# Eight products of 128 moving columns in place of two of 512 in a graph kernel's edge stage

## The chip, the cores and the metric

The kernel runs on one core of a Trainium2 chip. The metric is the device time of one execution in microseconds (us). The engines that matter here are TensorE (PE in the profile, its weight loads shown apart as PEld), VectorE (DVE), ScalarE (ACT) and SyncE (SP), which issues the DMAs.

## What is computed

Four graph layers over 512 nodes, each with 512 features. The 8192 edges (`src`, `dst`, sorted by `dst`) are the same in all of them. The part that matters here is what the edges give to each layer: layer 0 is sparse attention with 8 heads and one bias per edge and head, the others add or average neighbours.

```python
x, src, dst, edge_attr_8              # (512,512), (8192,), (8192,), (8192,8)
scores = einsum('ehd,ehd->eh', q[row], k[col]) * scale + bias
m = segment_max(scores, row);  p = exp(scores - m[row])
alpha = p / segment_sum(p, row)[row]
out = segment_sum(alpha[:, :, None] * v[col], row)
...
agg = segment_sum(x[src], dst)        # the later layers: the same edges, unweighted
```

## The kernel before

The kernel turns the edge list into dense 512x512 matrices, one for each of the 8 heads (the sum of exp(bias) over the edges from one node to another) and one with the count of edges. After that everything is dense products. The dense matrices are made in the **edge stage**, and the change is in it.

The edges come in 64 tiles of 128. The destination nodes come in 37 blocks of 14 (`BW`). A **slot** is one tile of edges meeting one block; there are 100 slots, in 25 groups of 4 (`GROUP`). For a slot the kernel needs, for each of the block's 14 nodes and 9 quantities (8 heads and the count, `KW`), a row over all 512 source nodes: 14 x 9 = 126 rows (`BROWS`). TensorE makes them as a product over the slot's 128 edges. The stationary side (126 columns, loaded as weights) holds each edge's weights in the place of its destination; it exists twice, as a high and a low part for precision (a = 0, 1). The moving side is a one-hot matrix, 128 edges x 512 sources. Both are fp32r. So a slot is two products, of the two stationary sides with the same 512 moving columns, summed in the same PSUM bank. In the profile the moving side is called `wide_rounded` and the stationary side `c_rounded`.

Which PSUM bank a slot adds to depends on its block, known only at run time. TensorE's sequencer reads the block numbers of two groups into registers (`choices`, L1379), waits until the block's bank has been cleared (`evacuated`), and computes the bank's address (an ALU operation and a fused register operation).

VectorE builds the operands: `one_hots` (L792, four per group) and `left_sides` (L798, one per group), in a ring of two groups (`RING`). It may write a ring place once the products that read it are done (`pair_mm`), and TensorE waits for `built` at each group. ScalarE copies each finished block out of PSUM (L483), clears its bank (L488), and SyncE writes the copy to its place by DMA (L287).

TensorE mixes into this stage the query, key and value projections (`qkv_step`, L1373): 48 plain fp32 products of 512 columns, each in the trace as two MATMUL records of two passes. The list `qkv_group` says after which group how many of them come: 7, 4, 3, then 2 after each of 13 groups, then 0, 2, 0, 2, 0, 2, 0, 2. So late in the stage two groups follow one another with no projection between them. The last group runs in a loop (one trip here) that ends with small table products. Behind the stage TensorE computes attention scores (L1447), transposes (L1461) and weighted sums (L1476), and then the rest of the layers.

Ahead of the stage the transposes of z (L1415) are copied out by ScalarE (L459), and the first projection waits for all four copies; the products of group 0 stand in that wait.

Of the kernel before, what the change touches and what calls it, by code (L numbers as in the profile page):

```python
# [24 lines left out]
NT = N // P  # L25
# [39 lines left out]
def gnn_kernel(nc, x, src, dst, bias, eps, cols, rows, wq, wk, wv, wo, w1_0, w2_0,  # L65
               wl_t, wr_t, w1_2, w2_2, w1_3t, w2_3t, out):
    ctx = ExitStack()
    with ctx:
# [76 lines left out]
        for name, words in (("mask", SLOTS * BW), ("bias", HP * P), ("src", P), ("dst", P), ("low", P),  # L145
# [24 lines left out]
        st_ring = c1_r[:, :, :].rearrange("p t n -> p (t n)")[:, 0:RING * GROUP * 2 * BROWS].rearrange(  # L170
            "p (g a w k) -> p g a w k", g=RING, w=BW, k=KW)
        hot_ring = wide_r[:, 0:RING * GROUP, :].rearrange("p (g s) n -> p g s n", g=RING)
# [1016 lines left out]
        def _(pe):  # L1189
            def tile(ap, t):  # L1190
                return ap[:, t * P:(t + 1) * P]
# [106 lines left out]
            def ks(a, n=NT):  # L1298
# [17 lines left out]
                             stop=True).then_inc(S["ends_mm"], 1)  # L1316
# [67 lines left out]
            def pairs(g, u, held):  # L1384

                pe.wait_ge(S["built"], g + 1)
                for k in range(GROUP):
                    pe.wait_ge(S["evacuated"], held[k])
                    to = acc[0:BROWS, bass.ds((held[k] & (ACC - 1)) * N, N)]
                    for a in range(2):  # L1390
                        last = nc.tensor.matmul(to, st_ring[:, u, 2 * k + a, :, :].rearrange("p w k -> p (w k)"),  # L1391
                                                hot_ring[:, u, k, :], start=False, stop=False, skip_group_check=True)
                    last.then_inc(S["pair_mm"], 1)

            def zeros(banks):
# [16 lines left out]
            for i, t in enumerate((0, 2, 1, 3)):  # L1412
                pe.wait_ge(*((S["z_ready"], t + 1) if t < 2 else (S["z_scalar"], t - 1)))
                for c in range(NT):
                    last = nc.tensor.transpose(tile(bank[Z_BANKS[c]], t), tile(z_sb[:, t, :], c), ident[:, :])  # L1415
                    if i == NT - 1:
                        last.then_inc(S["turned"], 1)
            for g in range(NG - 1):
                pairs(g, g % RING, held[GROUP * (g % 2):GROUP * (g % 2 + 1)])
                if g == 0:  # L1420
                    pe.wait_ge(S["t_ready"], NT)
                if g == 1:
                    pe.wait_ge(S["weights_read"], 1)
                for n, after in enumerate(qkv_group):
                    if after == g:
                        qkv_step(n)
                if g % 2 == 1 and g < NG - 2:
                    held = choices((g + 1) * GROUP, 2 * GROUP)
                if g == 2:
                    pe.wait_ge(S["ends_ready"], 1)  # L1430
                    trips = pe.value_load(rounds_i[0:1, 0:1], min_val=1, max_val=MAX_TRIPS)
            with nc.tensor.Fori(0, trips) as j:
                pe.wait_ge(S["rows_ready"], j + 1)
                pe.sem_inc(S["pair_steps"], 1)
                pairs(j + (NG - 1), 0, choices(FIXED))
                pe.wait_ge(S["qkv_ready"], LAST_V[0])
                pair_table(j + 1, slice(FIXED, SLOTS))
# [68 lines left out]
            for t in range(NT):  # L1506
                pe.wait_ge(S["att_ready"], 2 * NT - 1 if t == NT - 1 else 2 * t + 2)
                for c in range(NT):
                    if t == NT - 1 and c == NT // 2:
                        pe.wait_ge(S["att_ready"], 2 * NT)  # L1510
                    last = nc.tensor.transpose(tile(bank[c], t), tile(z_sb[:, t, :], c), ident[:, :])
# [24 lines left out]
            for k in range(NT):  # L1536
                pe.wait_ge(*reads("h1")[k][0])
                for i in range(2):
                    for m in range(NT):
                        nc.tensor.matmul(bank[m][:, :], tile(h1[k][0], m), c1s[k][i], start=(k == 0 and i == 0),  # L1540
                                         stop=False)
            pe.wait_ge(S["h_ready"], 2 * NT)
            turn(h_sb, 4, "turned")
            for k in range(NT):
                pe.wait_ge(*reads("h1")[k][1])
                for m in range(NT):
                    last = nc.tensor.matmul(bank[m][:, :], tile(h1[k][1], m), c1s[k][0], start=False,
                                            stop=(k == NT - 1))
# [102 lines left out]
```

## Time and profile before

| what | value |
|---|---|
| time, median of 2 runs (lowest to highest) | 397.99 us (396.95 to 399.02) |
| span of the profiled execution | 395.7 us |
| PE busy | 371.7 us (94%), 1781 matmuls |
| PEld busy | 282.1 us (71%), 1781 loads |
| DVE busy | 313.2 us (79%) |
| ACT busy | 171.5 us (43%) |
| L1391, the products of the slots | 200 matmuls, 58.2 us busy |
| L1373, the projections | 96 matmul records, 44.5 us busy |
| mean granted TensorE clock | 0.992 |

The span is that of one profiled execution, from its first to its last instruction; the runs' median is 2.3 us above it. A matmul's recorded duration is its latency, and consecutive matmuls overlap in the records. What one costs in a dense row is therefore the distance from one start to the next and not the mean duration.

### The profile page before, as it was taken

To read this page: it belongs to the slowest core of one execution; us is meant where nothing else is said; L and a number is where in the kernel's file an instruction comes from. 1 tells how busy PE (TensorE), PEld (TensorE's weight loads), DVE (VectorE), ACT (ScalarE), POOL (GpSimd) and SP (SyncE) were. 2 spreads that over 40 slices of the span, in tenths; PEclk is the share of its full clock that TensorE was granted. 3 is DMA by queue.
4 is the path that set the end of the run, shared out by engine and by line. 5 is a ranking of instruction groups with operands and counts; after the bars stand their busy time and mean duration, and the time that the engine had idled before them with its cause. 6 is when DMAs were issued, how large, how long until landed. Compare 5 with 4: busy or idle time off the path is not lost.

```text
span 395.7 us, 5097 instructions
## 1 busy us (share of the span) xinstructions
PE 371.7 (94%) x1781; PEld 282.1 (71%) x1781; DVE 313.2 (79%) x660; ACT 171.5 (43%) x287; POOL 4.2 (1%) x19
## 2 busy tenths in 40 slices
PE   2889999999988999999989999999799999999994
PEld 1555666666757888887768788887578878787873
DVE  5889999999947779997886978499875778488346
ACT  5664666444136224343467723361363531135320
POOL 4000000000000000000000000000000000000000
PEclk9999999999998999999999999999999999999998
DMA  7602444343226000056500230400420032000002
GB/s 240 247 1 69 157 154 135 104 133 110 73 85 208 2 2 1 2 188 243 206 2 1 100 114 14 198 2 0 134 81 0 2 116 96 2 0 0 2 2 104
DMA packets 16360, 32.92 MB, mean 83 GB/s; under 512 B 1360, under 2 KB 1488, under 8 KB 16336
## 3 DMA queue, kind: packets, MB, share of 16 engines
q1 hardware_dynamic: 15744, 32.25, 23.6%
q10 hardware_dynamic: 592, 0.36, 0.3%
q8 instruction: 15, 0.25, 0.3%
q14 instruction: 9, 0.07, 0.1%
HBM read 21.07 MB, written 1.05 MB: 56 GB/s over the span
## 4 chain that ended last, share of the span: by engine, by line
PE 78%; DVE 14%; ACT 4%; issue 3%; DMA 1%; DVEq 0%; ACTq 0%
PE acc L1391 11%; PE bank L1373 10%; PE bank L1476 7%; PE bank L1270 6%; PE bank L1271 6%; PE bank L1251 4%; PE acc L1251 4%; PE acc L1271 4%; PE acc L1270 4%; PE bank L1461 4%; PE acc L1447 3%; DVE big_rounded L652 2%; PE acc L1228 2%; PE bank L1228 2%; PE acc L1540 2%
## 5 line engine op out<-in xcount | busy, mean ns | idle before, releaser
L1391 PE MATMUL acc<-wide_rounded,c_rounded 128*126 128x512 f32 x200 | 58.2, 435 | 0.7 <-ACT acc L464 0.7
L1391 PEld LDWEIGHTS acc<-wide_rounded,c_rounded 128*126 128x126 f32 x200 | 37.2, 187 | 17.8 <-issue 10.7
L792 DVE TENSOR_SCALAR wide_rounded<-iota_f,picked 128x512 fp32r<-128x512 f32 x100 | 42.6, 482 | 2.1 <-issue 1.1
L483 ACT COPY z_sb<-acc 126x512 f32<-126x512 f32 x37 | 21.6, 585 | 44.9 <-PE acc L1391 36.2
L507 ACT ACTIVATE wide<-wide,low_col 128x512 f32<-128x512 f32 x32 | 21.3, 715 | 32.8 <-DVE low_col L905 32.8
L1476 PEld LDWEIGHTS bank<-v_sb,big 128*128 128x128 f32 x256 | 29.7, 192 | 4.7 <-issue 4.3
L625 DVE TENSOR_TENSOR wslot_rounded<-wslot,wide_rounded 128x512 fp32r<-128x512 f32 x24 | 16.2, 688 | 21.3 <-ACT wslot L377 21.3
L1476 PE MATMUL bank<-v_sb,big 128*128 128x65 f32 x256 | 31.6, 277 | 0.0
L798 DVE TENSOR_TENSOR c_rounded<-row_bc,wslot_rounded 128x1008 fp32r<-128x1008 bf16 x25 | 30.0, 1201 | 0.0
L1373 PE MATMUL bank<-t_sb,wslot 128*128 128x512 f32 x64 | 29.5, 594 | 0.5 <-ACT t_sb L459 0.5
L652 DVE TENSOR_TENSOR big_rounded<-big,big_rounded 128x1024 fp32r<-128x1024 f32 x24 | 29.1, 1222 | 0.4
L369 ACT ACTIVATE std<-mv,eps_c 128x1 f32<-128x1 f32 x20 | 5.8, 290 | 39.4 <-DVE mv L657 25.9
L905 DVE CUSTOM_DVE_ANT_0 wide<-acc,t_sb 128x512 f32<-128x512 f32 x32 | 20.7, 684 | 1.7 <-PE acc L1447 1.6
L917 DVE TENSOR_TENSOR big<-bank,big 128x512 f32<-128x512 f32 x32 | 20.6, 684 | 1.4 <-PE bank L1461 1.4
L1461 PE MATMUL bank<-ident,wide 128*128 128x128 f32 x128 | 18.3, 285 | 2.7 <-ACT wide L507 2.7
L1373 PEld LDWEIGHTS bank<-t_sb,wslot 128*128 128x128 f32 x64 | 12.0, 189 | 11.5 <-issue 9.6
L488 ACT COPY acc<-zero_c 126x512 f32<-126x512 f32 x33 | 19.4, 588 | 1.0
L1271 PE MATMUL acc<-big_rounded,wslot_rounded 128*128 128x512 f32 x48 | 18.7, 389 | 0.0
L1270 PE MATMUL acc<-big_rounded,wide_rounded 128*128 128x512 f32 x48 | 18.7, 389 | 0.0
L1461 PEld LDWEIGHTS bank<-ident,wide 128*128 128x128 f32 x128 | 15.0, 151 | 4.2 <-ACT wide L507 3.6
L374 ACT ACTIVATE wide_rounded<-bank,col 128x512 fp32r<-128x512 f32 x12 | 8.3, 694 | 17.4 <-PE bank L1271 17.4
L1373 PE MATMUL bank<-wslot,t_sb 128*128 128x512 f32 x32 | 15.0, 592 | 0.0
(314 smaller groups left out, 768.8 us busy)
## 6 DMA issues: line engine op xcount, KB each, us to landing
big<-z_sb SPq DMA_DIRECT2D x36, 252.0 KB
big<-in_w SPq DMA_DIRECT2D x4, 2048.0 KB, 7.8
x_sb<-in_x SPq DMA_DIRECT2D x8, 256.0 KB, 4.7
big<-in_w_3t SPq DMA_DIRECT2D x2, 1024.0 KB, 6.8
row_bc<-in_rows SPq DMA_DIRECT2D x7, 256.0 KB, 6.6
wslot<-in_wq SPq DMA_DIRECT2D x1, 1024.0 KB, 8.9
wslot<-in_wk SPq DMA_DIRECT2D x1, 1024.0 KB, 10.8
wslot<-in_wv SPq DMA_DIRECT2D x1, 1024.0 KB, 12.8
```

The costliest lines, as they stand in the source:

```text
L483: nc.scalar.copy(stage[0:BROWS, b % STAGES, :], a).then_inc(S["staged"], 1)
L507: nc.scalar.activation(e, e, ACT.Exp, bias=low_col[:, n // 4, h:h + 1], scale=-1.0).then_inc(S["e_ready"], 1)
L652: nc.vector.tensor_tensor(lo.rounded[:, part, :], lo.full[:, part, :], hi.rounded[:, part, :].bitcast(F32), ALU.subtract).then_inc(S[name ...
L792: nc.vector.tensor_scalar(hot_ring[:, u, k, :], iota_f[:, :], picked[:, 0, s0 + k:s0 + k + 1], None, ALU.is_equal)
L798: nc.vector.tensor_tensor(st_ring[:, u, :, :, :], mask[:, c, :, :].rearrange("p s a w -> p (s a) w").unsqueeze(3).broadcast_to([P, 2 * GRO ...
L1251: nc.tensor.matmul(bank[banks[m]][:, :], tile(a[0], m), r[0], start=(k == 0 and not started), stop=False)
L1270: nc.tensor.matmul(bank[b][:, :], tile(a[0], m), r[1], start=False, stop=False)
L1271: last = nc.tensor.matmul(bank[b][:, :], tile(a[1], m), r[0], start=False, stop=(k == len(terms) - 1))
L1373: ins = nc.tensor.matmul(to[:, :], left, right, start=(k == 0), stop=(k == NT - 1))
L1391: last = nc.tensor.matmul(to, st_ring[:, u, 2 * k + a, :, :].rearrange("p w k -> p (w k)"), hot_ring[:, u, k, :], start=False, stop=False, ...
L1461: last = nc.tensor.transpose(tile(bank[4 + a], t), tile(held_e[:, i % HELD, :], t), ident[:, :])
L1476: last = nc.tensor.matmul(o, by_head[:, t, h, m * P:(m + 1) * P], v_sb[:, t, h, :], start=(t == 0), stop=(t == NT - 1))
```

## The change

The two products of a slot become eight. The 512 source columns are cut into four tiles of 128; for each tile the two stationary sides are multiplied with the tile's 128 moving columns, into the same 128 columns of the same bank. The same sums are made. The order is tile outside, side inside, so the stationary side alternates from product to product. The semaphore update stands on the slot's last product, as before. Nothing else is changed.

```diff
                 for k in range(GROUP):
                     pe.wait_ge(S["evacuated"], held[k])
                     to = acc[0:BROWS, bass.ds((held[k] & (ACC - 1)) * N, N)]
-                    for a in range(2):
-                        last = nc.tensor.matmul(to, st_ring[:, u, 2 * k + a, :, :].rearrange("p w k -> p (w k)"),
-                                                hot_ring[:, u, k, :], start=False, stop=False, skip_group_check=True)
+                    for t in range(NT):
+                        for a in range(2):
+                            last = nc.tensor.matmul(tile(to, t),
+                                                    st_ring[:, u, 2 * k + a, :, :].rearrange("p w k -> p (w k)"),
+                                                    tile(hot_ring[:, u, k, :], t), start=False, stop=False,
+                                                    skip_group_check=True)
                     last.then_inc(S["pair_mm"], 1)
```

On TensorE, at the last slot of group 0 and the projections behind it (L1391 is the slot's product, L1373 a projection; REGISTER_ALU and ISA are the sequencer's register operations that give the bank's address), before:

```order
L1391 REGISTER_ALU
L1391 ISA
L1391 MATMUL acc<-wide_rounded,c_rounded 126x512 x2
L1373 MATMUL bank<-t_sb,wslot 128x512 x7
L1391 REGISTER_ALU
```

and of the change, at the same place:

```order
L1392 REGISTER_ALU
L1392 ISA
L1392 MATMUL acc<-wide_rounded,c_rounded 126x128 x2
L1392 ISA
L1392 MATMUL acc<-wide_rounded,c_rounded 126x128 x2
L1392 ISA
L1392 MATMUL acc<-wide_rounded,c_rounded 126x128 x2
L1392 ISA
L1392 MATMUL acc<-wide_rounded,c_rounded 126x128 x2
L1373 MATMUL bank<-t_sb,wslot 128x512 x7
L1392 REGISTER_ALU
```

Each slot has six more products and three more register operations, since each tile's address is worked out on its own. The projections keep their place. The instructions of the other engines keep their order.

## Rows read from the trace of the kernel before

**Rows 1.** Page, costliest groups: busy us, mean ns of one, idle before it

```profile
L1391 PE MATMUL acc<-wide_rounded,c_rounded 128*126 128x512 f32 x200 | 58.2, 435 | 0.7 <-ACT acc L464 0.7
L1391 PEld LDWEIGHTS acc<-wide_rounded,c_rounded 128*126 128x126 f32 x200 | 37.2, 187 | 17.8 <-issue 10.7
```

**Rows 2.** Chain that ended last, in order of time: start us, us, what

```profile
25.59 6.28 PE bank L1373 x14
31.86 1.88 PE acc L1391 x8
...
86.29 1.72 PE bank L1373 x4
88.00 3.69 PE acc L1391 x16
91.69 1.72 PE bank L1373 x4
93.41 3.72 PE acc L1391 x16
...
109.72 1.86 PE acc L1391 x8
...
114.55 0.89 PE acc L1447 x5
```

**Rows 3.** Groups of the stretch from 26 to 111.5 us, same columns as rows 1

```profile
L1391 PE MATMUL acc<-wide_rounded,c_rounded 128*126 128x512 f32 x192 | 55.8, 436 | 0.0
L792 DVE TENSOR_SCALAR wide_rounded<-iota_f,picked 128x512 fp32r<-128x512 f32 x92 | 39.2, 482 | 1.9 <-issue 1.1 <-PE acc L1391 0.8
L798 DVE TENSOR_TENSOR c_rounded<-row_bc,wslot_rounded 128x1008 fp32r<-128x1008 bf16 x23 | 27.6, 1201 | 0.0
L483 ACT COPY z_sb<-acc 126x512 f32<-126x512 f32 x36 | 21.0, 584 | 38.7 <-PE acc L1391 30.0 <-issue 4.4 <-DMA big<-z_sb 4.3
```

**Rows 4.** PEld timeline, transposes and first slot: start us, us, what, count

```profile
20.35 0.20 PEld L1415 LDWEIGHTS acc<-ident,z_sb 128*128 128x128 f32 x2 [2.14 <-issue]
20.52 0.25 PEld L1415 LDWEIGHTS bank<-ident,z_sb 128*128 128x128 f32 x2
20.74 0.25 PEld L1415 LDWEIGHTS acc<-ident,z_sb 128*128 128x128 f32 x2
...
22.05 0.30 PEld L1391 LDWEIGHTS acc<-wide_rounded,c_rounded 128*126 128x126 f32 x2
```

**Rows 5.** PEld timeline in the attention: same columns

```profile
126.31 1.86 PEld L1476 LDWEIGHTS bank<-v_sb,big 128*128 128x128 f32 x16 [0.36 <-issue]
```

**Rows 6.** Instructions of L1476: duration ns min/median/max

```profile
L1476 PEld LDWEIGHTS bank<-v_sb,big x256: 186/192/192, 126.3 to 180.5; 128*128 128x128 f32 x128
```

**Rows 7.** Timeline at group 0, PE and ACT: start us, us, what [idle before]

```profile
22.07 1.63 PE L1391 MATMUL acc<-wide_rounded,c_rounded 128*126 128x512 f32 x6
...
23.57 0.59 ACT L464 COPY acc<-zero_c 126x512 f32<-126x512 f32 x1
24.10 1.44 ACT L459 ACTIVATE t_sb<-bank,col 128x512 f32<-128x512 f32 x2
...
24.39 0.72 PE L1391 MATMUL acc<-wide_rounded,c_rounded 128*126 128x512 f32 x2 [0.69 <-ACT acc L464]
...
25.59 1.12 PE L1373 MATMUL bank<-t_sb,wslot 128*128 128x512 f32 x2 [0.47 <-ACT t_sb L459]
```

**Rows 8.** Instructions of L1391 on TensorE's sequencer: duration ns min/median/max

```profile
L1391 PEldq ALU_OP  x100: 32/32/42, 21.8 to 108.5; - x100
L1391 PEldq FUSED_REGOPS  x100: 46/46/46, 21.9 to 108.6; - x100
```

**Rows 9.** Instructions of L1379, the reading of block numbers, same columns

```profile
L1379 PEldq TENSOR_LOAD <-rows_u x13: 1287/2201/2724, 11.7 to 106.3; - x13
```

**Rows 10.** Busy us (count) of PE, PEld, DVE, ACT, POOL in stretches; granted clock, DMA share, GB/s

```profile
20.00:30.00 10.00, 8.46 (x35) 5.06 (x36) 8.69 (x20) 6.28 (x11) 0.00 (x0) 1.00 0.00 1
...
60.00:70.00 10.00, 10.00 (x35) 6.18 (x33) 9.93 (x19) 6.83 (x12) 0.00 (x0) 1.00 0.41 132
...
111.60:120.00 8.40, 6.19 (x46) 4.81 (x47) 5.76 (x18) 4.38 (x7) 0.00 (x0) 0.96 0.47 158
120.00:127.00 7.00, 6.59 (x40) 5.02 (x39) 4.91 (x13) 3.63 (x6) 0.00 (x0) 0.80 0.68 221
127.00:245.00 118.00, 115.42 (x711) 94.48 (x711) 97.52 (x210) 54.68 (x83) 0.00 (x0) 1.00 0.20 72
```

## The prediction

> **What bounds the kernel now.** I read three views in this order. The costliest groups put the slots' products at the top, with almost no idle time before them [rows 1]. The chain of waits says whether that matters: from 25.59 to 109.72 + 1.86 = 111.6 us it never leaves TensorE; it alternates between runs of L1391 and the four records of a projection step, and each starts where the other ends [rows 2]. The groups of this stretch say who else is near the limit. VectorE's hot operations in it have only 1.9 us of idle time before them, while ScalarE's copies wait 30.0 us for TensorE's products [rows 3]. A ten-microsecond piece in the middle shows PE busy for 10.00 us and DVE for 9.93 [rows 10]. So the edge stage is set by TensorE, with VectorE close behind, and what is added to a product here is added to the time. What is removed would come back only until VectorE binds.
>
> What does a product cost now? The chain has 16 products in 3.72 us [rows 2], 0.2325 us each, so a slot costs 0.465 us. The mean of 435 ns [rows 1] is latency and not what the row pays.
>
> **The change part by part.** A slot had 2 weight loads and 2 x 512 moving columns. It now has 8 weight loads and 8 x 128 moving columns. The columns are the same; six loads are added. The stationary sides alternate, so no load can be left out.
>
> *Streaming.* If a product's time were in proportion to its columns, 128 of them would take 0.2325 / 4 = 0.058 us, and eight 0.465 us: no change.
>
> *Loading.* With 512 columns a load lies beside the streaming of the product before it. With 128 it has only 0.058 us of cover. What must be known is how close two loads with their products can follow one another. No fp32r product of 128 columns is in the trace. The nearest rows:
>
> - The transposes of z, 128 columns moving and 128 loaded. Pairs of loads start at 20.52 and 20.74 us [rows 4]: 0.11 us from one to the next.
> - The weighted sums, fp32, 128 columns loaded and two passes of 65 moving. Sixteen loads take 1.86 us [rows 5], the last of them 0.192 [rows 6]: (1.86 - 0.192) / 15 = 0.111 us.
> - The first two loads of L1391 itself, where the first finds nothing to wait for: together 0.30 us [rows 4], one is 0.187 [rows 1], so the second starts 0.11 us after the first.
>
> All three say 0.11, though the moving sides differ. The same interval in kinds so unlike says that the load sets it. I take 0.112 us for a product. The low bound is the transposes' 0.109 (0.22 / 2 less rounding). The high bound comes from L1391's own rows. A plain fp32 record streams 2 x 512 columns in 1.72 / 4 = 0.430 us, 0.215 per pass, whereas an fp32r product takes 0.2325 [rows 2]: 0.0175 more. If that is a bubble between the end of a load and the start of a product, it comes on top, 0.112 + 0.0175 = 0.130. If it lies in the streaming, it hides under the load. I take the latter, because the loads are then the longer of two parallel things by 0.04 us.
>
> The Trainium skill, page "TensorE: Matmul & The Clock Gate", section "LDWEIGHTS (loading the stationary operand)", gives a load as its columns divided by 1.2 ns, 105 ns for 126; the rows agree. The same page's "Back-to-back issue gap" gives a sustained stream of load and product about 81 ns at 128 columns and 131 ns at 512; by that, as an estimate, a slot would be 0.65 us, and the time 416 us. This trace has 232 ns at 512 columns and nothing under 109 at 128, so I go by the rows.
>
> *The slot.* 8 x 0.112 = 0.896 us instead of 0.465, that is +0.431 us.
>
> *How many slots pay.* Group 0 stands in a wait. TensorE does three of its slots from 22.07, waits for ScalarE's clearing until about 24.2, does the fourth, and is idle again until the last copy of the transposes lets the first projection start at 25.59 [rows 7]. With the change its 32 products take 32 x 0.112 = 3.6 us and end at about 25.7: +0.1 us. Without that cover the group would cost 4 x 0.431 = 1.7. The other 24 groups are on the path: 96 x 0.431 = 41.4 us.
>
> *The sequencer.* A slot has three more register operations, 46 ns each [rows 8], 0.14 us. They lie beside the products, which take 0.896 us. I cost them at nothing.
>
> *VectorE.* Its work per group, 4 x 39.2 / 92 = 1.7 us for the one-hots plus 1.2 for the left sides [rows 3] and now and then a projection's copy, was 3.57 us in step with TensorE's 1.86 + 1.72. TensorE's group grows to 5.3 us, so VectorE now waits on `pair_mm`. Queued behind that wait are only its next builds and projection copies; it has up to 1.7 us per group to spare. In the double groups, with no projection between, TensorE takes 3.6 us a group against VectorE's 2.9: still covered. ScalarE's copies already waited 30 us and wait longer. What is late next is everything behind the stage: the last block's copy, its DMA and the scores all hang on the last product and move as one.
>
> *Sum.* 41.4 + 0.1 = 41.5 us. The span 395.7 becomes 437.2 us. The median of the runs is 2.3 us above the span, so **439.5 us**.
>
> **The rivals.**
>
> *A bubble behind every load.* 96 x 8 x 0.0175 = 13.4 us more: 452.9 us. For it: the fp32r rows are longer per column than the plain ones. Against: the plain fp32 rows show loads 0.111 apart with hardly any bubble. Chance 0.10.
>
> *TensorE's clock.* The granted clock is 1.00 through the edge stage and from 127 us on, where transposes and 65-column products alternate with 512-column ones; it falls where TensorE waits, to a mean of 0.80 from 120 to 127 us [rows 10]. The new stage has stretches of 7.2 us with only short products, four of them in the double groups. If the clock fell to its lower level in each and came back with the projections, half of some 7 us would be lost four times: about 14 us, 453 us. Against: the attention's short products kept it up. The skill (same page, "HAM oscillation") ties the drop to idle gaps, and none is made here. Chance 0.10.
>
> *The sequencer is late.* Reading the block numbers takes 2.2 us (12 times in the stage) [rows 9], and the queue must hold work for that long. It used to hold products of 0.23 us, now of 0.11 us. If it held only 12, 1.3 us, each reading would show 0.9: 11 us, 450 us. Against: the idle time in [rows 1] shows no trace of these readings today. Chance 0.06.
>
> *Switching sides costs what it costs today.* If 0.2325 us is not the streaming of 512 columns but the least time between two fp32r products with different weights, each of the eight costs it: 96 x (1.86 - 0.465) = 134 us, 531 us. For it: no fp32r product in the trace is closer. Against: the streaming explains 0.215 of it. Chance 0.03.
>
> *Not slower.* If the loads hide, streaming sets the pace: 8 x 0.058 = 0.465 us a slot, and the time stays at 398 us. The place is the interval between loads, and it decides: under (0.465 + 8 / 96) / 8 = 0.069 us the change is within 2%. For it: the first two loads of the transposes take 0.20 us together, where every later two take 0.25 at 0.11 apart, that is 0.14 each [rows 4]; so the second of all began 0.06 after the first. Against: those go into an empty engine. Chance 0.04.
>
> *The loads hide in part.* Midway between these 0.06 and 0.11, at 0.085, a slot costs 0.68 us, and the time is 397.99 + 96 x 0.215 = 419 us. For it speaks only that first pair; every later one is 0.11 apart. Chance 0.03. The skill's figure of 81 ns, above, would be this case.
>
> **How the numbers follow.** The forecast, loads set the pace, has 0.64 and by itself the range 437 to 443 us (an interval of 0.109 gives 96 x 8 x 0.003 = 2.3 less; a few tenths more per load or for the clock at the stage's edges give the rest). The cases at 450 to 453 hold 0.26 more. The range is 436 to 455 us; outside it lie 0.07 below and 0.03 above, with the little part of the clock's chance in which it stays down for longer. A difference of about 2%, 8 us, is what a measurement can tell from no change. Within it: 0.04, the case not slower. Faster by over 2%: 0.01, for what I do not see, since no rival shortens the stage. Slower by over 2%: the rest, 0.95.
>
> **What would show it.** In the profile after: 800 loads and 800 matmuls of the slots in place of 200; in the chain, a group's 32 products in 3.5 to 3.7 us instead of 1.86 for its 8; the projections between them still 1.72 us per four records. The first projection starts at 25.6 to 25.8 us, the first scores at about 156 us instead of 114.6 [rows 2]. VectorE's busy time is unchanged, with some 40 us of new idle time before L792, ended by the slots' products. The granted clock stays 1.00 in the stage. The rest from the first scores on is as long as before. It is wrong if products are 0.06 or over 0.125 apart, if idle time shows before TensorE's loads with the sequencer as its releaser, or if the clock is below 1.00 in the double groups.

## The result, and the profile after

| what | before | changed |
|---|---|---|
| median (lowest to highest) | 397.99 us (396.95 to 399.02, 2 runs) | 440.94 us (439.29 to 442.59, 2 runs) |
| ratio, 95% interval | | 1.106 (1.099 to 1.113) |
| both again, beside each other on one chip | 399.35 us (11 runs) | 440.57 us (436.84 to 442.49, 6 runs), 1.104 (1.099 to 1.109) |
| span of the profiled execution | 395.7 us | 441.1 us |
| mean granted clock in it | 0.992 | 0.98 |

The change costs 42.95 us. The forecast was 439.5 us, slower; the median is 1.4 us above it. Runs of one kernel differ by a few us, the longer ones at a lower mean granted clock.

The page's groups of the changed kernel (busy us, mean ns of one, idle time before) answer to [rows 1, 3]:

```profile
L1392 PEld LDWEIGHTS acc<-wide_rounded,c_rounded 128*126 128x126 f32 x800 | 91.2, 189 | 9.6 <-issue 9.6
L1392 PE MATMUL acc<-wide_rounded,c_rounded 128*126 128x128 f32 x800 | 98.5, 282 | 0.0
L792 DVE TENSOR_SCALAR wide_rounded<-iota_f,picked 128x512 fp32r<-128x512 f32 x100 | 47.0, 485 | 32.3 <-PE acc L1392 30.8
L483 ACT COPY z_sb<-acc 126x512 f32<-126x512 f32 x37 | 21.7, 586 | 84.1 <-PE acc L1392 77.2
```

There are 800 loads and 800 products where there were 200 of each. TensorE still has no idle time before them. VectorE's one-hots, at 1.9 us of idle time before [rows 3], now wait 30.8 us for TensorE.

The chain of waits in order of time (start us, us, what) answers to [rows 2]:

```profile
22.21 3.47 PE acc L1392 x32
25.68 6.07 PE bank L1373 x14
31.76 3.47 PE acc L1392 x32
...
107.68 3.47 PE acc L1392 x32
111.15 1.77 PE bank L1373 x4
112.92 6.99 PE acc L1392 x64
119.91 1.77 PE bank L1373 x4
...
147.96 3.48 PE acc L1392 x32
151.44 0.02 issue
```

A group's products take 3.47 us instead of 1.86, a double group's 6.99 instead of 3.72. The projections between them hold 1.77 us of the chain instead of 1.72. Added up over the chain, from group 1 on, the products of the 24 groups take 83.5 us instead of 44.5, and the 19 stretches of projections 36.2 instead of 35.25: 39.9 us more. The last product of the stage ended at 109.72 + 1.86 = 111.58 us [rows 2] and now ends at 147.96 + 3.48 = 151.44, which is 39.9 us later too. The spans differ by 45.4. So 5.5 us more were lost behind the stage, where the program is the same.

The stretches of the changed kernel (busy us and count of PE, PEld, DVE, ACT, POOL; granted clock, DMA share, GB/s) show where:

```profile
112.00:151.40 39.40, 39.40 (x308) 35.02 (x306) 23.00 (x40) 6.46 (x11) 0.00 (x0) 1.00 0.16 50
...
153.50:160.40 6.90, 6.69 (x29) 4.50 (x28) 3.49 (x10) 0.15 (x1) 0.00 (x0) 0.51 0.44 146
160.40:163.80 3.40, 1.62 (x13) 1.30 (x13) 2.32 (x7) 2.30 (x4) 0.00 (x0) 1.00 0.93 298
163.80:167.20 3.40, 3.40 (x17) 2.32 (x15) 1.48 (x5) 2.40 (x4) 0.00 (x0) 0.50 0.67 257
```

```profile
327.70:331.10 3.40, 3.40 (x10) 1.20 (x9) 2.62 (x14) 1.29 (x3) 0.00 (x0) 0.51 0.99 370
331.10:423.20 92.10, 91.97 (x398) 73.67 (x397) 60.85 (x110) 35.17 (x57) 0.00 (x0) 1.00 0.07 24
423.20:426.60 3.40, 3.40 (x9) 2.62 (x10) 0.00 (x0) 0.00 (x0) 0.00 (x0) 0.50 0.00 0
```

The clock is 1.00 throughout the stage, the double groups included. Behind it, it is at its lower level (1.2 GHz of 2.4) for 6.9 us, then for 3.4, and again for 3.4 at 327.7 and at 423.2. The weighted sums, whose loads began at 126.31 [rows 5], begin at 168.72:

```profile
168.72 1.86 PEld L1479 LDWEIGHTS bank<-v_sb,big 128*128 128x128 f32 x16 [0.36 <-DVE big L917]
```

That is 42.4 us later, so 2.5 of the 5.5 us were lost up to here, beside the first falls. The clock is not all of it. TensorE also waited for the last block's DMA (a piece of the chain, then a row of the timeline):

```profile
152.07 4.63 DMA big<-z_sb
```

```profile
156.79 1.12 PE L1488 MATMUL bank<-ident,big 128*128 128x128 f32 x4 [0.21 <-SPq L292]
```

The wait is 0.21 us here and 0.71 in the profile of the change repeated. In the kernel before, the same copy was issued at 112.23 us and the wait for it was over by 115.39, after 3.2 us; in these two profiles it was 4.7 and 4.1. Why it takes longer stays open. The other two falls stand beside the rest, 3.0 us; two falls of 3.4 us at half the clock can cost 3.4 at most. The weighted sums' loads have kept their own pace, 16 in 1.86 us.

### The profile page after: what moved, and what is told of

Same layout as the page of the kernel before. It is cut to its first block, busy times and chain, and to the rows that moved or that the text cites. A ratio compares the mean times of both kernels' runs of the same rounds, so it can differ in the third digit from the quotient of the medians.

```text
span 441.1 us, 6597 instructions
## 1 busy us (share of the span) xinstructions
PE 418.6 (95%) x2381; PEld 336.3 (76%) x2381; DVE 318.6 (72%) x660; ACT 172.4 (39%) x287; POOL 4.1 (1%) x19
## 4 chain that ended last, share of the span: by engine, by line
PE 80%; DVE 12%; ACT 3%; issue 2%; DMA 2%; DVEq 0%; SPq 0%
PE acc L1392 20%; PE bank L1373 10%; PE bank L1479 6%; PE bank L1270 5%; PE bank L1271 5%; PE bank L1251 4%; PE acc L1251 4%; PE acc L1271 3%; PE acc L1270 3%; PE acc L1450 3%; PE bank L1464 3%; DVE big_rounded L652 2%; PE acc L1228 2%; PE bank L1228 2%; PE acc L1543 2%
## 5 line engine op out<-in xcount | busy, mean ns | idle before, releaser
L1392 PEld LDWEIGHTS acc<-wide_rounded,c_rounded 128*126 128x126 f32 x800 | 91.2, 189 | 9.6 <-issue 9.6
L1392 PE MATMUL acc<-wide_rounded,c_rounded 128*126 128x128 f32 x800 | 98.5, 282 | 0.0
L792 DVE TENSOR_SCALAR wide_rounded<-iota_f,picked 128x512 fp32r<-128x512 f32 x100 | 47.0, 485 | 32.3 <-PE acc L1392 30.8
L1373 PE MATMUL bank<-t_sb,wslot 128*128 128x512 f32 x64 | 30.1, 602 | 0.0
L1373 PEld LDWEIGHTS bank<-t_sb,wslot 128*128 128x128 f32 x64 | 11.2, 191 | 9.6 <-issue 9.6
L1373 PE MATMUL bank<-wslot,t_sb 128*128 128x512 f32 x32 | 15.5, 605 | 0.0
```

The source lines that it names most:

```text
L792: nc.vector.tensor_scalar(hot_ring[:, u, k, :], iota_f[:, :], picked[:, 0, s0 + k:s0 + k + 1], None, ALU.is_equal)
L1373: ins = nc.tensor.matmul(to[:, :], left, right, start=(k == 0), stop=(k == NT - 1))
L1392: last = nc.tensor.matmul(tile(to, t), st_ring[:, u, 2 * k + a, :, :].rearrange("p w k -> p (w k)"), tile(hot_ring[:, u, k, :], t), start= ...
```

## The experiments

The load theory says: each product brings its own load of 126 columns, 0.11 us, and streaming 128 columns, 0.058 us, is too short to cover it. So the longer of load and streaming sets the interval from one product to the next.

**Same side four times in a row.** The loops are swapped.

```diff
-                    for t in range(NT):
-                        for a in range(2):
+                    for a in range(2):
+                        for t in range(NT):
```

> The same eight products per slot, with the loops swapped: one side with its four tiles, then the other. So three of four products use the side that is already loaded. Load theory (each product brings its own load, 0.110 us apart, whether the side is new or not): nothing changes, 441 us, 800 loads in the trace. Rival (the alternating of sides is what costs, and a load of the same side is left out or quicker): a slot falls toward the streaming of 0.465 us, 398 to 406 us.

439.45 us (4 runs, 436.3 to 444.1), ratio 1.101 (1.093 to 1.110), still 800 loads:

```profile
L1392 PEld LDWEIGHTS acc<-wide_rounded,c_rounded x800: 184/190/190, 21.8 to 151.0; 128*126 128x126 f32 x160
```

The columns behind the name are duration in ns (min/median/max) and the first and last start. The last load starts at 151.0 us, as in the changed kernel (151.1). It is not the alternating that costs. A side that is already in place is loaded again, at full price.

**Four products of 256 columns.** The tiles are 256 wide (`range(2)`, slices of 256).

> Four products of 256 columns per slot. Load theory (interval = the longer of load, 0.110, and streaming): streaming in proportion is 0.2325 / 2 = 0.116 us, a slot 0.465, 398 us; if the 0.0175 us that an fp32r product of 512 columns takes over a plain pass is fixed per product, 0.107 + 0.0175 = 0.125, a slot 0.50, 401 us. Rival 1 (every further product costs the same, (0.880 - 0.465) / 6 = 0.069 us): 2 x 0.069 x 96 = 13 us, 411 us. Rival 2 (load and streaming of one product stand partly behind each other: 0.055 + the streaming, which gives 0.110 at 128 columns too): 0.165 us apart, a slot 0.66, 417 us.

The chain of its profile:

```profile
86.69 1.72 PE bank L1373 x4
88.41 3.76 PE acc L1392 x32
92.17 1.72 PE bank L1373 x4
```

A double group's 32 products take 3.76 us, 0.1175 each. A slot costs 0.470 us against 0.465. Twice the loads cost next to nothing, since streaming of 0.116 us covers a load of 0.11. Both rivals (0.60 and 0.66 a slot) fall, and so does a fixed 0.0175 us per product: 0.125 was due then. That surplus of fp32r over a plain pass goes about in proportion to the columns (0.0175 us at 512, 0.010 at 256). The stage ends at 110.33 + 1.89 = 112.2 us, 0.6 later than before. The whole time is another matter: the median is 402.3 us (4 runs, 397.8 to 404.2) against 398.0 (7 runs, 396.6 to 402.6) for the kernel before beside them. The two runs at 404 have the lowest mean clocks, 0.973 and 0.975. These runs can't show a difference of 1 us; what the cut costs in the stage is read from the trace.

**Half of the side loaded.**

```diff
-    nc.tensor.matmul(tile(to, t), st_ring[:, u, 2 * k + a, :, :]...
+    nc.tensor.matmul(tile(to[0:63, :], t), st_ring[:, u, 2 * k + a, 0:7, :]...
```

> Eight products of 128 columns, with stationary sides of 63 columns in place of 126: the upper half of each block's rows is left out of the sums, so its time is that of half the weights loaded. Load theory: the load takes half, 0.055 us, and no longer sets the interval; then streaming does (0.058, or 0.071 if 0.0175 is fixed per product), or TensorE's sequencer, at 0.09 + 4 x 0.124 = 0.59 us a slot, 0.074 a product: 398 to 410 us. Rival 1 (a product of 128 columns has this interval whatever is loaded): 0.110, 441 us. Rival 2 (half of the load behind the streaming): 0.083, a slot 0.66, 417 us.

The upper half of the rows is left out of the sums. 415.8 us (1 run). Chain:

```profile
65.94 1.93 PE acc L1392 x32
67.87 1.77 PE bank L1373 x4
69.64 2.47 PE acc L1392 x32
```

Where the row is dense, 32 products take 1.93 us, 0.060 each: it was the load, and with half of it gone the streaming of 0.058 sets the pace. Rival 1 (0.110) and rival 2 (0.083) both fall. But other groups take 2.47 us, and the stage ended at 122.76 + 2.25 = 125.0 us. The waits of the stage (who waited for whom: us in total, times, longest):

```profile
PEld acc L1392 <- issue: 15.3, 32, 1.7
...
DVE wide_rounded L792 <- PE acc L1392: 8.1, 15, 1.6
...
PE acc L1392 <- DVE c_rounded L798: 1.8, 3, 0.9
```

The slow groups are those behind a reading of block numbers on TensorE's sequencer. The reading ahead of the group at 69.64 us (instructions of L1379 from 66 to 68 us):

```profile
L1379 PEldq TENSOR_LOAD <-rows_u x1: 2337/2337/2337, 66.9 to 66.9; - x1
```

It ends at 69.2 us, and the group behind it takes 2.47 us, 0.077 a product. From 45 to 90 us it is every second group, 2.2 to 2.7 us, each behind a reading; the ones between take 1.93 or 1.94. Late in the stage VectorE comes on the chain as well: having waited 8.1 us for the late products, it makes TensorE wait three times, 1.8 us in all, for its left sides. The longest of the waits for issue, 1.7 us, ended at 101.05 and is in part that; up to 95 us none is over 1.1.

**Side of 90 columns.** `to[0:90]` and 10 of the 14 nodes; the other 4 are left out of the sums.

> Eight products of 128 columns with stationary sides of 90 columns in place of 126; the last 4 of a block's 14 nodes are left out of the sums. The side of 126 gave 0.110 us between loads, the side of 63 gave 0.060, where streaming has 0.058. Load theory (columns loaded / 1.2 per ns, and about 0.005): 0.080, a slot 0.64, the stage's last product 96 x 0.175 = 17 us later than before, at about 128 us, span 413 to 417. Rival (the interval is half load, half streaming): 0.0375 + 0.055 = 0.093, a slot 0.74, the stage's end at 138 us.

```profile
60.28 2.54 PE acc L1392 x32
62.81 1.77 PE bank L1373 x4
```

2.54 / 32 = 0.079 us each, where 0.080 was expected and 0.093 by the rival. From 90 to 126 columns the interval grows from 0.0794 to 3.47 / 32 = 0.1084 us: 0.81 ns a column. The recorded load itself grows from 160 to 190 ns, 0.83 a column. Time 418.15 us (1 run), span 416.6, stage end at 127.70 + 2.54 = 130.2 us instead of the 128 expected: a few groups took 2.75, or 5.35 to 5.41 for a double one, rather than 2.54 and 5.08. These stand behind a reading of block numbers, too.

**Half side, 256 columns.** Was the idle time of the half side TensorE's sequencer? This one halves the products and the address calculations.

> Four products of 256 columns with sides of 63 columns (half the rows left out, as in the run with eight of 128). There the products stood 0.060 us apart where they were dense, 0.48 a slot, yet the stage ended at 124.9 us instead of 111.5, with 15.3 us of idle time before TensorE's loads in which no other engine was waited for. Theory (that is the sequencer: 0.09 + 4 x 0.124 = 0.59 us for a slot of eight products with four address calculations): with half the calculations and half the products it needs 0.34, under the streaming's 0.47, and the stage ends at 112 us with little idle time of that kind, span 396 to 402. Rival (narrow sides themselves delay something, a copy, a wait for the built operands): the stage ends at 120 us or later.

The stage's last product ended at 110.32 + 1.91 = 112.2 us, and the waits read

```profile
PEld acc L1392 <- issue: 10.7, 40, 0.4
```

against 9.6 us in the kernel before. The long ones are gone. So in the half-side kernel the sequencer was late: it reads block numbers for 2.2 us, and products 0.060 us apart seem to use up what stands in its queue meanwhile (the queue itself is in no view). In the change itself, at 0.1085, that does not happen: its loads wait 9.6 us for issue in the stage, as before, the longest wait is 0.2 us, and every single group takes 3.47 or 3.48 us, whether it stands behind a reading or not. The run's 403.2 us (1 run, span 401.7) has another cause: its clock fell four times behind the stage.

**Where the cover is.** Only group 0, or only group 1, multiplies tile by tile; `n` is 128 (`P`) there and 512 (`N`) elsewhere.

```diff
+                    n = P if type(g) is int and g == 0 else N     # or g == 1
+                    for t in range(N // n):
```

> Only group 0 multiplies tile by tile, the other 24 groups as before. Cover theory: its 32 products take 3.5 us instead of 1.9 and end within 0.2 us of ScalarE's last copy, so the first projection starts at 25.5 to 25.8 us (25.59 before) and the time is 398 us, +0.1. Rival (no cover): it starts 1.7 us later, 399.7 us. The run's own spread is larger than that, so the trace decides.

> Only group 1 multiplies tile by tile. It stands between projections. Theory: +1.66 us on the chain, the stage's last product ends 1.66 us later (113.2 us in place of 111.6), less what VectorE's lead changes; 399.7 us. Rival: VectorE, which was 9.93 of 10 us busy, sets the later groups anyway, and TensorE catches up with it: the last product ends less than 1 us later.

399.2 and 401.0 us (1 run each). The chain with group 0, and then with group 1:

```profile
20.08 0.41 PE acc L1419 x2
...
22.02 3.47 PE acc L1393 x32
25.49 6.08 PE bank L1373 x14
31.57 1.86 PE acc L1393 x8
...
109.49 1.85 PE acc L1393 x8
```

```profile
20.15 0.41 PE acc L1419 x2
...
25.36 6.28 PE bank L1373 x14
31.64 3.47 PE acc L1393 x32
...
111.13 1.86 PE acc L1393 x8
```

The count has to begin ahead of group 0, at the first transpose. In the kernel before that is

```profile
20.38 0.41 PE acc L1415 x2
```

From there, the stage's last product ends after 111.58 - 20.38 = 91.2 us before, 111.34 - 20.08 = 91.3 with group 0 tiled, and 112.99 - 20.15 = 92.8 with group 1 tiled. So the first costs 0.1 us, the second 1.6. Group 0's products fill the wait for ScalarE: group 1 begins 11.5 us behind the first transpose in all three. VectorE, though 9.93 of 10 us busy [rows 10], absorbed nothing of group 1's.

**Sixteen products of 64 columns.**

> Sixteen products of 64 columns per slot, full sides. Load theory: 16 loads 0.110 apart, a slot 1.76 us, 0.88 more than with eight: 441 + 96 x 0.88 = 525 us, less nothing, since group 0 is now longer than its wait (+3.5 us): about 528 us. Rival 2 (0.055 of the load plus the streaming of 0.027): 0.082, a slot 1.32, 483 us. The sequencer's 0.09 + 8 x 0.124 = 1.08 us a slot is under both.

679.3 us (1 run): far over every forecast. The stretches of its profile:

```profile
26.20:36.40 10.20, 10.20 (x32) 7.15 (x31) 3.14 (x8) 2.28 (x4) 0.00 (x0) 0.50 0.14 38
36.50:43.30 6.80, 6.80 (x41) 4.88 (x39) 1.99 (x3) 1.17 (x2) 0.00 (x0) 1.00 0.01 3
207.20:389.00 181.80, 181.80 (x770) 167.32 (x769) 32.12 (x54) 11.15 (x19) 0.00 (x0) 0.50 0.05 16
```

TensorE was busy all the time by the profile, and still the granted clock went to its lower level again and again, and stayed there from 207 us to the end of the stage. At full clock the loads are 0.110 us apart, as expected; at the lower one 24 of them from 209.82 us on take 5.24 us, one 0.34: (5.24 - 0.34) / 23 = 0.213.

**Eight products of 64 columns.** Full sides, half of each tile's columns; the other half of the source nodes is left out.

> Eight products per slot with full sides, each of the first 64 of its tile's 128 columns; half the source nodes are left out of the sums. So the loads are those of the changed kernel and the streaming is half. Load theory: 0.110 us apart as with 128, the stage ends at 151 us, 440 us, if the clock is granted in full. In the run with sixteen products of 64 columns the clock fell again and again in the stage. If that came from the short columns, it falls here too: loads 0.213 apart in these stretches, and with projections in between keeping it up part of the time the time is 460 to 560 us. If it came from the length of the stretches without a projection (7 us and more there, 3.5 us here in most groups), the clock stays and it is 440 us.

482.2 us (1 run). The chain shows the fall:

```profile
65.90 3.44 PE acc L1392 x32
69.34 1.80 PE bank L1373 x4
71.14 3.44 PE acc L1392 x32
74.58 3.07 PE bank L1373 x4
77.65 3.85 PE acc L1392 x32
```

```profile
60.00:74.00 14.00, 14.00 (x103) 11.77 (x101) 10.50 (x18) 6.14 (x11) 0.00 (x0) 1.00 0.30 95
75.00:78.40 3.40, 3.40 (x10) 1.85 (x8) 1.22 (x2) 0.00 (x0) 0.00 (x0) 0.50 0.24 80
```

Up to 75 us a group costs 3.44 us, the 3.47 of the changed kernel: half the columns save nothing, as the load theory has it. Then the clock falls, first for 3.4 us at a time and later for 44. The loads come at the pace of the changed kernel, and the stretches without a projection were no longer than there; the columns streamed with each load, 64 and not 128, are what differs. With 128 the clock was 1.00 through the stage in the profiles of the change, of its repeat and of the swapped loops. So the falls go with the shorter streaming, as one run each of eight and of sixteen products shows. Why the falls begin at 75 us here and not at the stage's start stays open.

**The falls behind the stage.** Two kernels got products that only serve the clock, where TensorE waits: `keep_warm(bank, count)`. The wait for `weights_read` moves up to its new place in both; the first `keep_warm` is in the changed kernel only.

```diff
             scores(0)
+            pe.wait_ge(S["weights_read"], 2)
+            keep_warm(5, 4)                       # the changed kernel only
             ...
             counts_turn(1)
+            pe.wait_ge(S["qkv_ready"], LAST_V[0] + 1)
+            keep_warm(6, 7)
```

> The changed kernel, with products that serve only TensorE's clock (bf16, 512 columns, into a free bank) where it waits behind the edge stage: 4 ahead of the wait for the last blocks' DMA, 7 ahead of the first transposes. In the changed kernel's profile the granted clock is 0.5 from 153.6 to 160.4 and from 163.8 to 167.2 us, and from the stage's last product to the steady attention it loses 2.6 us against the kernel before. Theory (the falls behind the stage come from TensorE's waiting there, and cost these 2.6 us): one of the falls goes or is shorter, 1 to 2 us less, 438.5 to 440 us. Rival (they come from the short products of the stage, or the added products are in the way): no gain, 441 to 442 us.

> The kernel before, with the 7 products ahead of the first transposes alone. There the clock is 0.5 from 119.4 to 122.8 us, behind 1.8 us of waiting. Theory: with the wait filled the clock stays, 1 to 2 us less, 396 to 397 us against 398. Rival: the added products delay the transposes by what they overrun the wait, up to 0.5 us, and the clock falls all the same: 398.5 us.

The changed kernel with them: 439.02 us (436.4 to 442.1, 6 runs), ratio to the kernel before 1.102 (1.097 to 1.108), where the change alone had 1.106 and 1.104: the intervals overlap. The kernel before with them: ratio 1.001 (0.998 to 1.003), no gain. In its profile the clock had fallen already ahead of the added products:

```profile
111.00:114.20 3.20, 2.77 (x26) 2.43 (x24) 0.91 (x5) 2.07 (x3) 0.00 (x0) 1.00 0.23 74
114.20:117.60 3.40, 3.40 (x15) 2.23 (x16) 1.77 (x4) 0.00 (x0) 0.00 (x0) 0.50 0.38 98
```

The added products run from 118.54 us on, behind this fall. The fall at 119.4 us that the theory went by is not there, but this one is. So the theory that 1 to 2 us were to be had falls for the kernel before. For the changed one it is undecided. Its profile, too, has a fall at 154.4 us, ahead of the added products, then full clock up to 325 us: 3.4 us of low clock behind the stage where the first profile had 10.3. And 439.0 us lies in the forecast of 438.5 to 440. But the change again, below, had runs from 436.8 to 442.5 without any added product. No version here beats the kernel before.

**The change again.**

> The changed kernel again, unaltered, for how much its time moves with the granted clock alone. Theory (what is beyond the stage's 39.9 us in the first profile is the clock's falls behind the stage, which differ from run to run): runs from 436 to 444 us, the long ones with the lower mean clock, median 439 us; kernel before 396.5 to 401 on the same chip. Rival (the falls belong to the change): all runs at 440 and above.

Median 440.57 us, six runs. The shortest, 436.84, has a mean clock of 0.992; 439.63 and 439.86 have 0.985 and 0.988; the three from 441.28 to 442.49 have 0.977 to 0.980. The kernel before does the same beside it: 396.68 us at 0.996, 402.57 at 0.979. The rival, all runs at 440 us or more, falls: three are under it. What the clock withheld, (1 - mean clock) x span, is 435.3 x 0.008 = 3.5 us in the shortest run and 441.0 x 0.02 = 8.8 in the longest, an estimate that covers 5.3 of the 5.7 us between them. The falls come and go in one and the same kernel. The median, 440.6, is above the 439 I expected.

## Why the prediction was right

**What bounds the kernel: right.** The chain stays on TensorE from one end of the stage to the other, and group 1 alone, tiled, moved the stage's end by the whole 1.6 us that its products are longer.

**0.112 us a product: right in mechanism, 3% high.** It is 0.1085 (3.47 / 32) in single groups and 0.109 (6.99 / 64) in double ones. The three rows of 0.11 were the right ones, and of the two ends I gave for it the low one, 0.109, was the value. I had rounded it up; over 768 products that is 2.5 us. That the load sets it and not something else was an argument from three unlike rows; the sides of 63, 90 and 126 columns now show it: 0.060 (streaming binds), 0.079, 0.1085, and so does the cut into 256 columns, 0.1175 with the same load. The Trainium skill, page "TensorE: Matmul & The Clock Gate", section "LDWEIGHTS (loading the stationary operand)", has columns / 1.2 ns; by that, 36 columns are 30 ns, and the runs have 29. Its 81 ns for a stream of loads and products at 128 columns ("Back-to-back issue gap", which names no type) does not hold for these fp32r products: they stand 108.4 to 109.2 ns apart in every group of the stage.

**The slot, 0.431 us more, over 96 slots: 41.4 us forecast.** The products give 83.5 - 44.5 = 39.0, and the projections 1.0, which I had not seen: each of their 19 stretches is 0.05 us longer in the chain behind short products. Together 39.9 us, 1.5 less than forecast.

**Group 0 at 0.1 us: right.** The run with it alone shows 0.1 us. It was hidden by ScalarE's copies, with nothing to spare: the last copy ends at 25.43 us, and the loads of the first projection, behind the last of the 32 products' loads, start at 25.48.

**The sequencer at nothing: right, with less room than it seems.** The loads' idle time for issue in the stage is 9.6 us before and after. The rival "the sequencer is late" had the mechanism right and fell for the interval: at 0.060 us a product, with half the side, nearly each reading of block numbers did make the group behind it longer, by 0.25 to 0.8 us.

**VectorE: right in that it does not bind, wrong in two sizes.** 30.8 us of idle time before L792, ended by TensorE's products; I had said some 40. And its busy time is not unchanged: 318.6 us instead of 313.2. Of that, 4.3 us are the stage's 92 one-hots, 43.5 us instead of 39.2 at nearly the same mean duration (485 ns, 482 before), so their records overlap less. 3.3 us more stand in its wait for the small tables' products at the stage's end (6.9 us instead of 3.6).

**What is behind the stage moves as one: wrong in size.** It was forecast as long as before. In the profile it is 5.5 us longer, nearly all at the places where the clock fell, and 0.2 us of it TensorE's wait for the last block's DMA. The sum had taken the clock of the kernel before as given, with one fall behind the stage. Repeats show that these falls are not fixed to the place or the kernel.

**The median 2.3 us above the span: wrong.** Each run's time is 1.2 to 1.6 us above its own span. The 2.3 came from a profiled execution that was the shorter one of two; of the changed kernel the longer one was profiled, and its span of 441.1 us is 0.2 above the median.

**That the forecast hit so closely is in part luck.** The span was 3.9 us over the 437.2 forecast: 1.5 less in the stage and 5.5 more behind it. The term of 2.3 us was 2.5 too high, and so the median is only 1.4 us from the forecast.

**The rivals.** The bubble behind every load: not there, the interval is 0.1085 us and not 0.130, and 256 columns showed 0.1175. Switching at 0.2325 each (by its own terms 532 us, not 531), loads hidden in whole or in part: neither. The clock in the double groups: granted in full there. But this rival deserved its chance, for with half the columns in each product it came true, without an idle gap, at a cost far beyond what I had worked out: 41 us with eight products. With sixteen, a mean clock of 0.759 over 677.8 us is 163 us withheld, enough for the 151 over the load theory's 528.

## What to carry to other kernels

The cost of cutting a product into shorter ones is read from how far apart two weight loads can start. If the streaming of a piece is longer than that (here 256 columns, 0.1175 us against 0.11), the cut is nearly free; if it is shorter, every product costs a load, and keeping the same weights does not help, since they are loaded again. Then ask whether TensorE is the bound at each place: the same cut cost 0.1 us in a group that stood in a wait and 1.6 us in one that did not.

## What the runs showed that I had not expected

TensorE's clock did not follow the profile's busy share. With products of 64 columns behind full loads, PE was busy for 181.8 of 181.8 us by the profile, and the granted clock was 0.50 for all of it; with 128 columns and the same loads it was 1.00 for the whole of the stage. In kernels with the same products behind the stage the clock fell there for 3.4 to 10.2 us, at times that differ from run to run. The spread of one kernel's times, up to 6 us, goes with it.

Reading four or eight block numbers into registers holds TensorE's sequencer for 1.0 to 3.0 us. That cost nothing with products 0.1085 us apart; it made a few groups longer at 0.079, and at 0.060 nearly every group behind a reading.
